# Flamingo block, one core: the second cross-attention's theta projection is moved to the input stage and kept in DRAM

## The chip, the cores and the metric

The kernel runs on one core of a Trainium2 chip. The metric is the device time of one execution in microseconds, the median of several runs. The profile is one execution recorded by the hardware. Its engines are TensorE (PE; its weight loads are PEld), VectorE (DVE), ScalarE (ACT), GpSimd (POOL) and SyncE (SP), which here only issues DMAs.

## What is computed

The block has four stages on `x` of 8 batches x 256 rows x 512 columns, with a context `ctx_2048` of the same shape. Each adds its gated result to x.

```python
x = x + tanh(g_xattn[0]) * L0_xattn(ctx, ctx, layernorm(x), ssm_kernel, D, 8)
x = x + tanh(g_ffn[0])   * L0_ffn(layernorm(x), w1, b1, w2, b2)          # int8-like, GELU
x = x + tanh(g_xattn[1]) * L1_xattn(layernorm(x), ctx, ...)
x = x + tanh(g_ffn[1])   * L1_ffn(x, w1, g1, w2, g2, w3, g3)             # ternary weights
```

The third line is the one that the change touches (input1 is the normalised x, input2 is the context, per batch 256 x 512):

```python
theta_x = einsum('ld,bdt->btl', theta_w, input2) + theta_b
phi_x   = einsum('ld,bdt->blt', phi_w, input1) + phi_b[:, None]
scores  = einsum('btl,bls->bts', theta_x, phi_x)
p       = softmax(scores, axis=-1)
g_x     = einsum('ld,bdt->btl', g_w, input1) + g_b
t_x     = einsum('bts,bsl->blt', p, g_x)
h       = relu((t_x - mean) * rsqrt(var + eps) * ln_gamma + ln_beta)     # mean, var over t and l
return einsum('ol,blt->bot', out_w, h) + out_b[None, :, None] + input2
```

`theta_x` depends on the context and two weights alone, not on x.

## The kernel before

The program is written out by hand for each engine, with semaphores between them. Each engine runs its own list of instructions in order, and a wait holds up all that stands behind it on that engine. There are 16 tiles of 128 rows (two to a batch), each 128 x 512 in float32, and 8 PSUM banks of 128 x 512.

**Input stage.** SyncE issues x and ctx in four groups of four tiles, 1 MB each (L306, L307), between them the small inputs (L309 to L312), then the convolution kernel's store to DRAM (`kpad_d`, L315), two bias loads (L316, L317) and the four 1 MB pieces of the first feed-forward's weights (L323). The third and fourth of these overwrite ctx in SBUF, so they wait until GpSimd has reversed its tiles (`c_rev`). For each tile t GpSimd reverses a piece of ctx (L456), ScalarE normalises x (L607), TensorE transposes ctx (L972) and x (L978), ScalarE copies the first out of PSUM (L615) and VectorE the second (L1305). VectorE makes the statistics of a group (L1295) between its copies. Then VectorE finds the largest magnitudes of the weights (L1323), ScalarE quantises them in four chunks of four instructions (L632), GpSimd or VectorE casts them (L481, L1342), TensorE transposes them (L963) and VectorE copies them out (L1332). ScalarE also issues the first loads of the convolution's matrices (L641).

**Convolution**, first feed-forward: L998 is the convolution's matmul, the first instruction of the next stage on TensorE. These stages are not touched.

**Second cross-attention.** Its eight batches are pipelined by one. TensorE's body for batch b is: `project(b + 1)` with theta (L1129, two float32 matmuls that the trace shows as four), phi (L1134) and g (L1142); `out_proj(b - 1)` (L1200); transposes of the probabilities (L1153); the product with g (L1182); `scores(b + 1)` (L1149); a small matmul for the mean (L1194). ScalarE copies theta (L851) and phi (L853) out with their bias, does the relu (L863), copies the transposed probabilities (L872) and takes the exponentials (L858). VectorE: statistics and normalisation of batch b + 2 (L1527, L1532, L1537), g out of PSUM (L1583), the residual (L1627, L1633), statistics of the product (L1601 to L1607), row maxima of the scores (L1589), the layer norm (L1612 to L1620), division of the exponentials (L1594, L1596). The weights of the four projections are loaded (L385, L386) and transposed (L1098) just before the stage, the context is loaded a second time (`ctx3`, L375), and the ternary weights are transposed between (L963, L1564 to L1569). `project(0)` stands among these.

**Names.** `arena` is one SBUF block out of which most tensors are cut, `turn`, `late` and `cols3` are further ones, `ps` is PSUM. `c_tr` and `q_tr` count transposed tiles of ctx and x, `c_out` and `q_out` copied ones, `pj_ready` finished projections, `th_out` copied projections, `sc_ready` finished score banks.

## Time and profile before

| | |
|---|---|
| median of 3 runs | 825.09 us (824.92 to 825.59) |
| span of the profiled execution | 821.3 us |
| TensorE busy | 680.4 us, 83% |
| VectorE busy | 707.5 us, 86% |
| ScalarE busy | 546.6 us, 67% |
| GpSimd busy | 359.2 us, 44% |
| input stage, up to the convolution's first matmul | 55.15 us |
| second cross-attention, theta(0) to the last scores | 465.5 to 590.3 us |

The span is from the first to the last instruction of one execution. The profiled execution's own time is not among the runs shown, and the distance from its span to the median of the runs is 3.8 us. Busy shares are averages over stages with different limits, so they are read by stretch. Where an instruction waited, its row in the timeline ends in brackets: the idle time before it, and who ended it. The start of DMA issues is also in the timeline, on SPq or ACTq. How long a transfer takes from its issue to its landing is in the DMA tables.

### The profile page before, as it was taken

Reading aid. Unit: us, or ns where it says so; the run is one execution under the profiler, and the core shown is the slowest. Engines: PE = TensorE matmul, PEld = TensorE weight load, DVE = VectorE, ACT = ScalarE, POOL = GpSimd, SP = SyncE. Lnnn points to the kernel's source line nnn. Section 1 sums busy time; section 2 is a strip of 40 time slices with the busy share of each in tenths; the row PEclk is TensorE's granted clock in tenths of the full one; section 3 lists DMA queues with packets and bytes.
Section 4 is the critical chain, followed back from the end, with each engine's and each line's share of the span. In section 5 each row is a group of like instructions: output and inputs, shape, how many; then the busy total and the mean of one; then the engine's idle time right before and its main releaser. Section 6 shows DMA issues by size and latency. Waiting matters only on the chain.

```text
span 821.3 us, 11803 instructions
## 1 busy us (share of the span) xinstructions
PE 680.4 (83%) x3440; PEld 405.8 (49%) x3476; DVE 707.5 (86%) x1044; ACT 546.6 (67%) x880; POOL 359.2 (44%) x436
## 2 busy tenths in 40 slices
PE   3669777597778738998969789999888999999996
PEld 3457555475555534443424655555534444444442
DVE  3867999999999974897789668888999999999993
ACT  3757777357677466989663554444557888888884
POOL 4649666387672240011753301010145556555552
PEclk9969999899999887998989999999999999999999
DMA  8925656077776220212865200000000000000000
GB/s 310 324 104 179 202 179 206 26 215 219 228 220 217 103 102 1 91 64 83 328 204 158 78 1 2 0 0 0 0 1 14 23 15 26 13 26 13 26 26 27
DMA packets 50048, 83.18 MB, mean 101 GB/s; under 512 B 6433, under 2 KB 19489, under 8 KB 48865
## 3 DMA queue, kind: packets, MB, share of 16 engines
q1 hardware_dynamic: 45664, 74.43, 27.1%
q10 hardware_dynamic: 4352, 8.39, 3.5%
q8 instruction: 14, 0.23, 0.1%
q14 instruction: 18, 0.14, 0.1%
HBM read 68.04 MB, written 14.76 MB: 101 GB/s over the span
## 4 chain that ended last, share of the span: by engine, by line
DVE 39%; PE 31%; ACT 12%; issue 12%; POOL 2%; DMA 2%; DVEq 1%; SPq 0%; ACTq 0%; POOLq 0%
DVE arena L1367 14%; PE ps L1075 5%; DVE turn L1360 5%; PE ps L1040 4%; ACT arena L922 3%; PE ps L1182 3%; PE ps L1149 3%; DVE arena L1646 3%; DVE q L1651 2%; PE ps L1129 2%; DVE arena L1734 2%; PE ps L1142 2%; PE ps L1134 2%; PE ps L1153 1%; DVE sw L1323 1%
## 5 line engine op out<-in xcount | busy, mean ns | idle before, releaser
L998 PE MATMUL ps<-arena 128*128 128x288 f32 x640 | 165.4, 417 | 44.8 <-ACT arena L670 33.5
L998 PEld LDWEIGHTS ps<-arena 128*128 128x128 f32 x640 | 122.3, 194 | 87.6 <-ACT arena L670 30.2
L1367 DVE TENSOR_REDUCE arena<-turn 128x2048 f32 (+1 forms) x32 | 123.8, 3872 | 0.0
L1220 PE MATMUL ps<-arena 128*128 128x512 bf16 x496 | 114.0, 380 | 10.7 <-ACT arena L898 7.6
L567 POOL TENSOR_TENSOR arena<-arena 128x512 f32<-128x512 f32 x64 | 87.8, 1374 | 68.9 <-DVE arena L1734 68.8
L473 POOL TENSOR_TENSOR arena<-arena 128x1024 f32<-128x1024 f32 x32 | 63.2, 1976 | 52.3 <-PE ps L998 51.7
L1220 PEld LDWEIGHTS ps<-arena 128*128 128x128 bf16 x512 | 47.5, 98 | 71.4 <-issue 14.2
L1075 PE MATMUL ps<-arena 128*128 128x512 bf16 x251 | 60.0, 402 | 10.8 <-DVE arena L1523 7.9
L1357 DVE TENSOR_TENSOR turn<-arena 128x1280 f32<-128x1280 f32 x32 | 53.5, 1671 | 14.7 <-ACT arena L670 12.6
L1238 PE MATMUL ps<-arena 128*128 128x512 bf16 x248 | 61.1, 386 | 0.8 <-ACT arena L914 0.5
L658 ACT ACTIVATE arena<-arena 128x512 f32<-128x512 f32 (+1 forms) x32 | 20.0, 629 | 60.0 <-DVE turn L1360 59.9
L1040 PE MATMUL ps<-arena 128*128 128x512 bf16 (+1 forms) x249 | 57.0, 385 | 2.3 <-ACT arena L769 1.7
L902 ACT ACTIVATE arena<-ps,q 128x512 f32<-128x512 f32 x64 | 41.7, 674 | 14.8 <-PE ps L1220 14.8
L1734 DVE SCALAR_TENSOR_TENSOR arena<-ps,q,arena 128x512 f32<-128x512 f32 x64 | 47.5, 744 | 0.7 <-ACT arena L902 0.5
L1075 PEld LDWEIGHTS ps<-arena 128*128 128x128 bf16 x256 | 25.9, 102 | 44.5 <-issue 17.7
L769 ACT ACTIVATE arena<-ps,b,s 128x512 f32<-128x512 f32 x64 | 45.3, 794 | 3.8 <-PE ps L1040 2.7
L858 ACT ACTIVATE arena<-ps,nmx 128x512 f32<-128x512 f32 x32 | 21.8, 685 | 33.7 <-DVE nmx L1589 33.0
L1740 DVE TENSOR_REDUCE q<-arena 128x1 f32<-128x512 f32 x64 | 42.1, 676 | 1.7 <-POOL arena L567 1.6
L908 ACT ACTIVATE arena<-arena,q 128x1024 int16<-128x1024 f32 x32 | 35.0, 1141 | 12.3 <-DVE q L1753 12.3
L1443 DVE TENSOR_REDUCE hmax<-arena 128x1 f32<-128x2048 f32 x15 | 34.0, 2277 | 9.9 <-ACT arena L769 9.9
L1040 PEld LDWEIGHTS ps<-arena 128*128 128x128 bf16 x256 | 24.9, 99 | 32.5 <-ACT arena L769 3.1
L667 ACT ACTIVATE arena<-ps 128x1024 f32<-128x1024 f32 x32 | 32.2, 1008 | 11.1 <-PE ps L998 11.1
(206 smaller groups left out, 1499.4 us busy)
## 6 DMA issues: line engine op xcount, KB each, us to landing
arena<-in_L_ffn_w SPq DMA_DIRECT2D x72, 256.0 KB, 4.2
arena<-kpad_d ACTq DMA_DIRECT2D x16, 512.0 KB, 4.5
late<-in_L_ffn_w SPq DMA_DIRECT2D x24, 256.0 KB, 4.3
tern_d<-late SPq DMA_DIRECT2D x48, 128.0 KB, 4.1
arena<-in_x SPq DMA_DIRECT2D x4, 1024.0 KB, 11.8
arena<-in_ctx SPq DMA_DIRECT2D x4, 1024.0 KB, 13.2
arena<-in_L_ffn_w SPq DMA_DIRECT2D x4, 1024.0 KB, 10.6
x_d<-arena SPq DMA_DIRECT2D x4, 1024.0 KB, 4.1
```

The costliest lines, as they stand in the source:

```text
L473: pool.tensor_tensor(dst[:, :, 0:32].rearrange("p r (d i) -> p r d i", d=4), a, shifted, ALU.mult)
L567: pool.tensor_tensor(hg[:, s, sl], hh[:, s, sl], g3[:, sl], ALU.mult).then_inc(S["hg_done"], 1)
L769: act.activation(hid[:, q, f, :], ps[:, f % 4, :], ACT.Gelu, bias=b1[:, f:f + 1], scale=s1[:, f:f + 1]).then_inc(S["gelu_done"], 1)
L998: last = pe.matmul(ps[:, 4 * s + lo, 0:NB * PAIRS], toep[:, u, (lo - li) * P:(lo - li) * P + P], kv[:, s, li, :], start=(li == 0), stop=(l ...
L1040: last = pe.matmul(ps[:, f % 4, :], fw1T[:, k, f * P:(f + 1) * P], xqT[:, k, ds(L * r, L)], start=(k == 0), stop=(k == LB - 1))
L1075: return pe.matmul(ps[:, 2 * j + f // 8, :], hq[:, r % 2, f, j * P:(j + 1) * P], fw2T[:, f, :], start=(f % 8 == 0), stop=(f % 8 == 7))
L1220: last = pe.matmul(ps[:, 3 + 2 * j + c % 2, :], xq4T[:, s, 4 * j + k, :], w[:, k, c * L:(c + 1) * L], start=(k == 0), stop=(k == LB - 1))
L1238: last = pe.matmul(ps[:, 7, :], hqT[:, f, :], bw3T[:, f, :], start=(f == 0), stop=(f == FT - 1))
L1357: v.tensor_tensor(prod[u][:, :, 0:5, :], bass.AP(yd.tensor, yd.offset, [yp, [YW, ROWS], [16, 5], [1, 8]]), bass.AP(qd.tensor, qd.offset, [ ...
L1367: v.tensor_reduce(qT[:, :, ds(HD * h, HD)], prod[u].rearrange("p r t i -> p r i t"), AX, ALU.add).then_inc(S["o_done"], 1)
L1734: v.scalar_tensor_tensor(out=hh[:, s, c * L:(c + 1) * L], in0=ps[:, 5 + c % 2, :], scalar=q4[:, 12 + 2 * s:13 + 2 * s], in1=sil[:, c, :], ...
L1740: dv.done(v.tensor_reduce(q4[:, 32 + c:33 + c], hg[:, s, c * L:(c + 1) * L], AX, ALU.max, apply_absolute_value=True))
```

## The change

- `theta_w` and `theta_b` are loaded behind the small inputs, ahead of the second group of x. TensorE transposes the two halves of theta_w after tile 1, and ScalarE copies them to `thw` after its copy of tile 2.
- `theta(b)` is computed on TensorE from the ctx that the input stage has in SBUF, after the transposes of tile 2b + 4, and for b = 6 and 7 at the end. It uses banks 1 to 3 in turn. ScalarE copies theta(b) with its bias to one of two buffers of `thT` (`th_copy`) after its copy of tile 2b + 5, and b = 6 and 7 at the end. From b = 2 on, this waits until the store of theta(b - 2) has landed (`th_moved`).
- SyncE stores the eight results to `th_d` in DRAM: 0 to 3 behind the second piece of the feed-forward weights, 4 and 5 behind the third, 6 and 7 behind the fourth. The third and fourth piece now also wait for the thetas that read the ctx tiles they overwrite.
- Before the second cross-attention theta(0) and theta(1) are loaded back; theta(b) for b of 2 and more is issued when the scores of b - 2 are done. `scores(b)` waits for the load. The projection and its copy are gone from there, and six weights are transposed there, not eight.
- GpSimd's first pairs of the convolution and the feed-forward's first weight transposes wait until theta is done with ctx and with the banks. Some semaphores are merged, to stay within their number, and `dynamic_dma_scratch_size` is set to 1024, which makes room in SBUF.

Cut to its core (numbers of semaphore counts that only shift are left out):

```diff
+        thT = sb("thT", [P, 2, L])
+        thw = sb("thw", [P, 4, P])
+        th_d = nc.dram_tensor("th_d", [NB, P, L], F32, kind="Internal").ap()
...
@@ SyncE, after the small inputs of group 0
+                    sp.dma_start(thw[:, 0:2, :], theta_w_d.rearrange("l (d k) -> l d k", d=2)).then_inc(S["w3_in"], 16)
+                    sp.dma_start(cols3[:, 0:1], theta_b_d.rearrange("(p o) -> p o", o=1)).then_inc(S["late_in"], 16)
...
+            def th_store(b):
+                sp.wait_ge(S["th_out"], b + 1)
+                sp.dma_start(th_d[b], thT[:, b % 2, :]).then_inc(th_moved[b % 2], 16)
+
             for c in range(4):
                 if c >= 2:
                     sp.wait_ge(S["c_rev"], G * (c + 1))
+                    sp.wait_ge(S["pj_ready"], 2 * c + 2)
                 sp.dma_start(raw[c].rearrange("p (j k) -> p j k", j=4), w1c[c]).then_inc(w_in[c], 16)
+                for b in ((), range(4), range(4, 6), range(6, 8))[c]:
+                    th_store(b)
...
+            def th_load(b):
+                sp.dma_start(thT[:, b % 2, :], th_d[b]).then_inc(th_moved[b % 2], 16)
+
+            for p in range(2):
+                sp.wait_ge(th_moved[p], 16 * NB // 2)
+            th_load(0)
+            th_load(1)
...
+            for b in range(2, NB):
+                sp.wait_ge(S["sc_ready"], 4 * (b - 1))
+                th_load(b)
...
@@ GpSimd
             pool.wait_ge(S["c_out"], NT)
+            pool.wait_ge(S["pj_ready"], NB)
...
@@ ScalarE
+            def th_copy(b):
+                act.wait_ge(S["pj_ready"], b + 1)
+                if b >= 2:
+                    act.wait_ge(th_moved[b % 2], 16 * (b // 2))
+                act.activation(thT[:, b % 2, :], ps[:, 1 + b % 3, :], ACT.Identity, bias=cols3[:, 0:1]).then_inc(S["th_out"], 1)
+
...
                 normalise_tile(x0[:, t % 4, :], t, t, S["xn0_ready"])
                 c_copy(t)
+                if t == 2:
+                    act.wait_ge(S["w3_tr"], 1)
+                    act.activation(thw[:, 2:4, :].rearrange("p a b -> p (a b)"), ps[:, 0, 0:2 * P], ACT.Copy).then_inc(S["w3_out"], 1)
+                    act.wait_ge(S["late_in"], 16)
+                if t >= 5 and t % 2 == 1:
+                    th_copy((t - 5) // 2)
+            for b in (NB - 2, NB - 1):
+                th_copy(b)
...
             def proj_out(b, p):
-                act.wait_ge(S["pj_ready"], 3 * b + 1)
-                act.activation(thT[:, p, :], ps[:, 0, :], ACT.Identity, bias=cols3[:, 0:1])
...
@@ TensorE
+            def theta(b):
+                pe.wait_ge(S["w3_out"], 1)
+                pe.wait_ge(c_in[b // 2], 16)
+                if b >= 3:
+                    pe.wait_ge(S["th_out"], b - 2)
+                for d in range(2):
+                    last = pe.matmul(ps[:, 1 + b % 3, :], thw[:, 2 + d, :], ctx_nat[:, 2 * b + d, :], start=(d == 0), stop=(d == 1))
+                last.then_inc(S["pj_ready"], 1)
...
                 last.then_inc(S["q_tr"], 1)
+                if t == 1:
+                    pe.wait_ge(S["w3_in"], 16)
+                    for d in range(2):
+                        last = pe.transpose(ps[:, 0, d * P:(d + 1) * P], thw[:, d, :], identf[:, :])
+                    last.then_inc(S["w3_tr"], 1)
+                if t >= 4 and t % 2 == 0:
+                    theta((t - 4) // 2)
+            for b in (NB - 2, NB - 1):
+                theta(b)
             for c in range(4):
                 pe.wait_ge(S["wqb_ready"], c + 1)
+                if c == 0:
+                    pe.wait_ge(S["th_out"], NB)
...
             def project(b, p):
                 pe.wait_ge(S["x3_done"], 2 * b + 2)
-                for d in range(2):
-                    last = pe.matmul(ps[:, 0, :], wT3[:, d, :], ctx3[:, ds(2 * b + d, 1), :].rearrange("p a t -> p (a t)"),
-                                     start=(d == 0), stop=(d == 1))
-                last.then_inc(S["pj_ready"], 1)
...
+            def scores(b, p, loaded):
+                pe.wait_ge(th_moved[p], 16 * (NB // 2 + loaded))
```

ScalarE in the input stage, tiles 7 to 9: before, a normalisation and a copy alternate.

```order
L615 ACTIVATE arena<-ps 128x4x128 [waits c_tr]
L607 ACTIVATE turn<-arena,shift2,rstd2 128x512 [waits q_tr,rs0]
L615 ACTIVATE arena<-ps 128x4x128 [waits c_tr]
L607 ACTIVATE turn<-arena,shift2,rstd2 128x512 [waits q_tr]
L615 ACTIVATE arena<-ps 128x4x128 [waits c_tr]
```

After, on the same engine for the same tiles (L628 is the normalisation, L636 the copy, L642 the copy of theta):

```order
L636 ACTIVATE arena<-ps 128x4x128 [waits c_tr]
L642 ACTIVATE thT<-ps,cols3 128x512 [waits pj_ready]
L628 ACTIVATE turn<-arena,shift2,rstd2 128x512 [waits q_tr,rs0]
L636 ACTIVATE arena<-ps 128x4x128 [waits c_tr]
L628 ACTIVATE turn<-arena,shift2,rstd2 128x512 [waits q_tr]
L636 ACTIVATE arena<-ps 128x4x128 [waits c_tr]
L642 ACTIVATE thT<-ps,cols3 128x512 [waits th_moved0,pj_ready]
```

A copy of theta now stands behind every odd tile, and the third one (the last row) also waits for a DMA, the first store.

SyncE's queue from the last group of ctx to the first ternary weights, before:

```order
L307 DMA arena<-in_ctx 128x4x512
L315 DMA kpad_d<-arena 32x640 [waits d_added]
L316 DMA b<-in_L_ffn_b 128x16x1
L317 DMA b2b<-in_L_ffn_b 128x512
L323 DMA arena<-in_L_ffn_w 128x4x512 x2
L323 DMA arena<-in_L_ffn_w 128x4x512 [waits c_rev] x2
L332 DMA arena<-in_L_ffn_w 128x512 [waits c_tr]
```

And after (L332 is now the feed-forward weights, L326 the store of theta):

```order
L309 DMA arena<-in_ctx 128x4x512
L319 DMA kpad_d<-arena 32x640 [waits d_added]
L320 DMA b<-in_L_ffn_b 128x16x1
L321 DMA b2b<-in_L_ffn_b 128x512
L332 DMA arena<-in_L_ffn_w 128x4x512 x2
L326 DMA th_d<-thT 128x512 [waits th_out] x4
L332 DMA arena<-in_L_ffn_w 128x4x512 [waits pj_ready,c_rev]
L326 DMA th_d<-thT 128x512 [waits th_out] x2
L332 DMA arena<-in_L_ffn_w 128x4x512 [waits pj_ready,c_rev]
L326 DMA th_d<-thT 128x512 [waits th_out] x2
L343 DMA arena<-in_L_ffn_w 128x512 [waits c_tr]
```

The stores stand between the weight loads, and the third and fourth load wait for finished thetas too.

## Rows read from the trace of the kernel before

**Rows 1.** Chain of waits, four stretches: start us, us, what it was spent on.

```profile
4.01 9.64 DMA arena<-in_x
...
465.67 1.77 PE ps L1129 x4
...
542.96 0.12 PE ps L1194 x2
543.08 1.82 PE ps L1129 x4
...
558.73 0.12 PE ps L1194 x2
```

**Rows 2.** Timeline, attention: start us, us, engine, line, operation, idle before.

```profile
543.00 0.69 DVE L1589 TENSOR_REDUCE nmx<-ps 128x1 f32<-128x512 f32 x1 [0.17 <-PE ps L1149]
...
547.66 0.48 DVE L1596 TENSOR_SCALAR arena<-arena,rrec 128x512 f32<-128x512 f32 x1
...
550.70 1.00 DVE L1537 TENSOR_SCALAR arena<-arena,mv,rstd 128x512 f32 x2 [0.50 <-POOL rstd L430]
...
553.16 1.41 DVE L1633 SCALAR_TENSOR_TENSOR arena<-turn,tg,arena 128x512 f32 x2
555.34 0.70 DVE L1601 BATCH_NORM_STATS2 bn<-ps 128x6 f32<-128x512 f32 x1 [0.77 <-PE ps L1182]
```

**Rows 3.** Busy time of a stretch: last three are clock, DMA share, GB/s.

```profile
32.50:35.00 2.50, 2.19 (x17) 1.72 (x17) 1.19 (x2) 2.50 (x5) 1.24 (x2) 1.00 1.05 404
```

**Rows 4.** Timeline, input stage: TensorE's and ScalarE's instructions for tiles.

```profile
20.72 0.60 PE L978 MATMUL ps<-identf,turn 128*128 128x128 f32 x4
...
27.91 0.58 ACT L615 ACTIVATE arena<-ps 128x512 f32<-128x512 f32 x1
...
28.39 0.81 ACT L607 ACTIVATE turn<-arena,shift,rstd 128x512 f32<-128x512 f32 x1
...
35.00 0.66 PE L978 MATMUL ps<-identf,turn 128*128 128x128 f32 x4
...
35.49 0.60 PE L972 MATMUL ps<-identf,arena 128*128 128x128 f32 x4
```

**Rows 5.** Timeline, from the last tile to the convolution's first matmuls.

```profile
36.14 0.59 ACT L615 ACTIVATE arena<-ps 128x512 f32<-128x512 f32 x1
...
36.64 0.48 ACTq L641 DMA_DIRECT2D arena<-kpad_d  x1
...
40.49 7.68 ACT L632 ACTIVATE turn<-arena,iw 128x512 int16<-128x512 f32 x12 [3.67 <-DVE iw L1327]
...
48.30 0.74 DVE L1342 CAST turn<-turn 128x2048 bf16<-128x2048 int16 x1
...
55.15 11.24 PE L998 MATMUL ps<-arena 128*128 128x288 f32 x39 [1.71 <-DVE arena L1332]
```

**Rows 6.** VectorE's waits from 495.7 to 590.3: us in total, times, longest.

```profile
DVE bn L1601 <- PE ps L1182: 3.6, 5, 0.9
...
DVE nmx L1589 <- PE ps L1149: 1.0, 6, 0.2
```

**Rows 7.** DMA issues by target: count, KB each, median us to landing.

```profile
out_x<-arena SPq DMA_DIRECT2D x16, 256.0 KB, 2.0
...
turn<-in_L_ffn_w SPq DMA_DIRECT2D x2, 1024.0 KB, 4.8
...
kpad_d<-arena SPq DMA_DIRECT2D x1, 80.0 KB, 12.2
...
gates<-in_g_xattn SPq DMA_DIRECT2D x1, 1.0 KB, 7.4
```

**Rows 8.** Timeline of SyncE's queue: the issue of b2b.

```profile
18.53 8.62 SPq L317 DMA_DIRECT2D b2b<-in_L_ffn_b  x1
```

**Rows 9.** L323's first two loads: issue ns, starts, then landing min/median/max.

```profile
L323 SPq DMA_DIRECT2D arena<-in_L_ffn_w x2: 435/704/972, 27.2 to 27.7; - x2
...
DMA to landing us min/median/max: 7.1/8.5/10.0
```

More of the change, by code:

```diff
@@ L127, in flamingo_gated_block @@
         xnb = cut(64, 2 * 2 * L).rearrange("p (s d l) -> p s d l", s=2, d=2)
-        thT = cut(72, 2 * L).rearrange("p (s t) -> p s t", s=2)
         phx = cut(76, 2 * L).rearrange("p (s t) -> p s t", s=2)
@@ L248, in flamingo_gated_block @@
         w_in = [sem(f"w_in{s}") for s in range(4)]
-        w2_in = [sem(f"w2_in{s}") for s in range(2)]
+        th_moved = [sem(f"th_moved{s}") for s in range(2)]
         traw_in = [sem(f"traw_in{s}") for s in range(4)]
@@ L353, in _ @@
                 sp.wait_ge(tint_out[c], 16 * 3 * FT // 4)
-            sp.dma_start(raw2[0], w2c[0]).then_inc(w2_in[0], 16)
+            sp.dma_start(raw2[0], w2c[0]).then_inc(w_in[0], 16)
             for g in range(NG):
@@ L367, in _ @@
                     sp.wait_ge(S["w2_used"], c - 1)
-                sp.dma_start(raw2[c % 2], w2c[c]).then_inc(w2_in[c % 2], 16)
+                sp.dma_start(raw2[c % 2], w2c[c]).then_inc(w_in[c % 2], 16)
             for g in range(NG):
@@ L382, in _ @@
                          tern_d[2].rearrange("r p n -> p r n")).then_inc(tern_in[1], 16)
-            for j, w in enumerate((theta_w_d, phi_w_d, g_w_d)):
+            def th_load(b):
[4 more added lines that the diff above has]
+            th_load(1)
+            for j, w in ((1, phi_w_d), (2, g_w_d)):
                 sp.dma_start(w3raw[:, 2 * j:2 * j + 2, :], w.rearrange("l (d k) -> l d k", d=2)).then_inc(S["w3_in"], 16)
             sp.dma_start(w3raw[:, 6:8, :], out_w_d.rearrange("(o p) l -> p o l", o=2)).then_inc(S["w3_in"], 16)
-            sp.dma_start(cols3[:, 0:1], theta_b_d.rearrange("(p o) -> p o", o=1)).then_inc(S["late_in"], 16)
             sp.dma_start(cols3[:, 1:2], phi_b_d.rearrange("(p o) -> p o", o=1)).then_inc(S["late_in"], 16)
@@ L409, in _ @@
             pool.nop().then_inc(S["kv_ready"], 2)
-            pool.memset(kpad[:, 0:NPAD], 0.0).then_inc(S["kz"], 1)
-            pool.memset(identf[:, :], 0.0).then_inc(S["ident_zeroed"], 1)
-            pool.memset(identb[:, :], 0.0).then_inc(S["ident_zeroed"], 1)
+            po.done(pool.memset(identf[:, :], 0.0))
+            po.done(pool.memset(identb[:, :], 0.0))
+            pool.memset(kpad[:, 0:NPAD], 0.0).then_inc(S["consts_set"], 1)
             pool.memset(mean_w[:, :], 1.0 / P).then_inc(S["consts_set"], 1)
@@ L418, in _ @@
                 pool.memset(rms_w[:, n:n + 1], value).then_inc(S["consts_set"], 1)
-            pool.wait_ge(S["ident_zeroed"], 2)
+            po.wait()
             for m in (identf, identb):
@@ L831, in _ @@
                     act.activation(ath[:, :], ath[:, :], ACT.Ln).then_inc(S["ath_ready"], 1)
-            act.wait_ge(S["w3_tr"], 1)
-            act.activation(wT3[:, :, :].rearrange("p a b -> p (a b)"), ps[:, 0:2, :].rearrange("p a b -> p (a b)"),
-                           ACT.Copy).then_inc(S["w3_out"], 1)
+            act.wait_ge(S["w3_tr"], 2)
+            act.activation(wT3[:, 2:8, :].rearrange("p a b -> p (a b)"),
+                           ps[:, 0:2, :].rearrange("p a b -> p (a b)")[:, 2 * P:8 * P], ACT.Copy).then_inc(S["w3_out"], 1)
             act.wait_ge(S["late_in"], 7 * 16)
@@ L955, in _ @@
             pe.nop().then_inc(S["y_ready"], 2)
-            pe.wait_ge(S["consts_set"], 8)
+            pe.wait_ge(S["consts_set"], 9)
             def weight_T(up, src, dst):
@@ L1096, in _ @@
             pe.wait_ge(S["w3_in"], 64)
-            for n in range(8):
+            for n in range(2, 8):
                 last = pe.transpose(ps[:, n // 4, (n % 4) * P:(n % 4 + 1) * P], w3raw[:, n, :], identf[:, :])
@@ L1106, in tern_T @@
                 if k == 3:
-                    pe.wait_ge(S["w3_out"], 1)
+                    pe.wait_ge(S["w3_out"], 2)
                 if k >= 4:
@@ L1144, in project @@
                 last.then_inc(S["pj_ready"], 1)
-            def scores(b, p):
-                pe.wait_ge(S["th_out"], b + 1)
+            def scores(b, p, loaded):
+                pe.wait_ge(th_moved[p], 16 * (NB // 2 + loaded))
+                pe.wait_ge(S["th_out"], NB + b + 1)
                 for k in range(4):
@@ L1186, in attn_body @@
                 if nxt:
-                    scores(b + 1, 1 - p)
+                    scores(b + 1, 1 - p, loaded)
                 if nxt:
@@ L1196, in out_proj @@
             def out_proj(b, copied):
-                pe.wait_ge(S["th_out"], copied)
+                pe.wait_ge(S["th_out"], NB + copied)
                 pe.wait_ge(S["relu_done"], b + 1)
@@ L1206, in _ @@
                 pe.wait_ge(*brought_out(k, S["bT_act"], S["bT_dve"], tern_on_dve))
-            scores(0, 0)
-            attn_body(0, 0, True, False)
+            scores(0, 0, 1)
+            attn_body(0, 0, True, False, 1)
             with pe.Fori(0, NB // 2 - 1) as i:
                 for u in range(2):
-                    attn_body(2 * i + 1 + u, (1 + u) % 2, True, True)
+                    attn_body(2 * i + 1 + u, (1 + u) % 2, True, True, i + 2)
             attn_body(NB - 1, 1, False, True)
@@ L1581, in gx_copy @@
             def gx_copy(b, p):
-                v.wait_ge(S["pj_ready"], 3 * b + 3)
+                v.wait_ge(S["pj_ready"], NB + 2 * b + 2)
                 v.tensor_tensor(gx[:, p, :, :], ps[:, 2, :].rearrange("p (b l) -> p b l", b=4),
```

14 lines of the change are left out of this document (7 added, 7 removed).

## The prediction

> **What bounds the kernel now.** I read the page's slices first, then the chain of waits, then two stretches instruction by instruction: the input stage (0 to 55 us), which the change loads, and the second cross-attention (465 to 590 us), which it relieves.
>
> In the attention stage the chain runs on TensorE alone: from one batch's last small matmul (L1194) to the next is 558.73 - 542.96 = 15.77 us, and inside it the theta projection (L1129) takes 1.82 us; the first projection, among the weight transposes, 1.77 us [rows 1]. So the first guess for what is taken off is 8 x 1.8 = 14 us. But VectorE is nearly as full: in the same period it waits 0.77 us at L1601 for TensorE's product and 0.17 us at the last row maximum (L1589); the 0.50 us at L1537 is a wait for GpSimd and stays [rows 2].
>
> The input stage is the other end. The DMA engines bring in 8 MB of x and ctx and 4 MB of weights, at full share and 404 GB/s where the queue is never empty [rows 3], and the normalise, transpose, copy-out loop over 16 tiles takes 35.00 - 20.72 = 14.28 us for ten tiles, 2.86 us for two [rows 4]. After it ScalarE quantises the first feed-forward's weights, and the long convolution starts at 55.15 us [rows 5]. From there on every stage waits for the one before, so each us that this start is late stays in the time.
>
> **The change, part by part.**
>
> *Taken out of the attention stage.* Projections 0 and 1: 1.77 + 1.7 us. Both are on TensorE's chain, and the engines behind it have room (VectorE's work of attention body 0 is light), so 3.5 us are gained before body 1. In bodies 1 to 6 TensorE alone could go from 15.77 to about 14.0 us. VectorE's chain decides instead. From the fourth row maximum (543.00) to the end of the residual update (553.16 + 1.41) are 11.57 us with its fixed wait in it; the next L1601 could start there, at 554.5, where it now starts at 555.34 [rows 2]. From L1601 on, the row maxima lose only their 0.17 us. So a period gives back its VectorE idle and no more: over 495.7 to 590.3 us that is 3.6 us at L1601 and 1.0 us at L1589 [rows 6], 4.6 us in six bodies, not 10.6. TensorE then waits for the normalised probabilities: they are ready 547.66 + 0.48 - 543.00 = 5.1 us after the fourth row maximum begins [rows 2], and it now waits for them where it waited for nothing. Sum: **-8.1 us**. ScalarE's eight theta copies there go too, but it waits anyway. The loads th_load(b) are issued two scores ahead, some 28 us, and 256 KB lands in a few us [rows 7]: nothing. Two transposes fewer of the attention weights lie beside the end of the second feed-forward matmul: nothing. The merged constant semaphores, and the smaller DMA scratch, which no DMA of this kernel uses: nothing.
>
> *Put into the input stage.* (a) Two more DMAs before the second x group. Its issue is now at 4.01 us behind six others, so one issue costs at most 0.67 us, and its landing (9.64 us later) starts the chain of the input stage [rows 1]. I take 1.0 us, between 0.3 and 1.5.
>
> (b) TensorE computes theta(b) after the transposes of tile 4, 6, ... 14, and ScalarE copies it out after each odd tile. This ties two tiles into one loop: transpose of the even tile (0.49 us to the next issue), theta 1.72, transposes of the odd tile of ctx 0.60, wake-up 0.05, the copy-out (27.91 to 28.39) 0.48, theta's copy-out of 128x512 with a bias, 0.6 from start to start by that same row, then the next even tile's normalisation 0.81 [rows 4], 0.05 again. Together 4.8 us for two tiles against 2.86. Transposes of tile 8 would then be at 20.72 + 1.0 + 2 x 4.8 = 31.3 us, and ScalarE ready for theta's third copy at 31.3 + 3.3 = 34.6.
>
> (c) That third copy needs the first store done (two thT buffers). SyncE issues the store behind b2b, which blocks the queue from 18.53 for 8.62 us [rows 8], and two 1 MB loads issued at 27.2 and 27.7 us, which landed 7.1 and 10.0 us later, the second at 37.7 [rows 9]. Is the store behind them in time as well as in order? Every small transfer in this queue was: 1 KB took 7.4 us, the 80 KB store kpad_d 12.2 us, behind megabytes [rows 7]. So the first store lands at 37.7 + 1.0 + 0.7 = 39.4 us and ScalarE stands 4.8 us, with the tiles behind it, and through them the transposes, VectorE's copies of q and GpSimd's reversals. The 0.7 us is 256 KB at the 404 GB/s of rows 3.
> The Trainium skill ("DMA: Bandwidth & Descriptors", Anatomy of one DMA) fits a transfer by itself as about 2.0 us plus its bytes at 436 GB/s, an estimate of 2.6 us for 256 KB; by that alone the store would be done at 32 us and step (c) would be nothing. The same page (Queues, rings and completion order) says that on each DMA engine descriptors are consumed in ring order, which is what the rows of small transfers show, so the sum goes by the rows.
>
> (d) From the stall: transposes of tile 10 at 39.4 + 0.6 + 0.8 + 0.05 = 40.9, tile 14 at 50.5 (now 35.00), theta(5) ends at 52.7. Only then may SyncE issue the third weight load, since it overwrites ctx, and the fifth store stands behind it: 52.7 + 4.8 (1 MB in an idle queue) + 0.7 = 58.2 us [rows 7]. Theta's last two copies wait for it and its neighbour: 59.4. Before, ScalarE's queue had issued its convolution loads (36.64 + 0.48) 0.4 us after the end of its last copy (36.14 + 0.59), so quantising starts at 59.8 to 59.9. Twelve pieces take 7.68 us: 67.6. VectorE's cast (48.30 before) follows, and the convolution starts 55.15 - 48.30 = 6.85 us after the cast: 74.4 us [rows 5]. Before, the quantising waited for VectorE's maxima; now those (10.6 us from 54.4) are done at 65. Sum: 74.4 - 55.15 = **+19.3 us**.
>
> *Total.* +19.3 - 8.1 = +11.2 us. The profiled execution spans 821.3 us, and the median of the runs is 825.09 us, 3.8 us round it that the change does not touch. Forecast: 821.3 + 11.2 + 3.8 = **836.3 us**.
>
> **The rivals.**
>
> 1. *The stores do not queue.* If a store issued at 28.5 us lands about 2.0 us later, as the output stores do in an idle queue [rows 7], (c) is zero. Tile 14 is then at 21.7 + 5 x 4.8 = 45.7, theta(5) ends at 47.9, the copies at 52.7 behind theta(7), the third quantised chunk at 60.8, the convolution starts at 67.7: +12.5, so 829.5 us. Against it stand the small transfers of 7 to 12 us. Chance 0.15.
>
> 2. *The attention stage gives all 14 us.* Then 836.3 - 6 = 830.3 us. It needs VectorE to lose what it does not lose in the diff; only its waits can go. Chance 0.06. Its opposite, in which TensorE's new wait for the probabilities and for the relu comes into VectorE's loop, gives 3.5 us only: 841 us. The relu is ready some 3.4 us after the fourth row maximum, TensorE wants it at 3.6, so this is near, but VectorE's path has over 1 us before it needs TensorE. Chance 0.07.
>
> 3. *Faster: theta disappears under the loads.* The input stage is fed by DMA, TensorE and ScalarE have gaps, and the convolution's start needs the weights more than the transposes. If the start is late only by (a), the time is 825.1 + 1.0 - 8.1 = 818 us. It turns faster if the input stage loses less than 8.1 us. For it: TensorE idles in that stage. Against it: the loop in (b) is fixed by the order on two in-order queues, and its sum without any stall, 5 x 1.94 = 9.7 us, is over 8.1. Chance 0.04.
>
> 4. *The change does less than it says*, losses and gains cancelling within 2 us: 0.02.
>
> **The numbers.** Forecast 0.66, rival 1 0.15, rival 2 0.06 and its opposite 0.07, rival 3 0.04, rival 4 0.02. The bounds of (a), of a wake-up more or less in (b) (5 x 0.2) and of the store's landing (1 us) give the forecast itself 833.5 to 839. The range reaches to rival 1 and to the opposite of rival 2: 829.5 to 841.5. Faster or slower counts from 0.2%, 1.7 us, about what a measurement of this kernel can tell from no change: faster 0.04, same 0.02, slower 0.94.
>
> **What would show it.** In the profile after: ScalarE idle about 5 us before theta's third copy, put down to a DMA; another wait before its seventh; two tiles every 4.8 us between; the convolution's first matmul near 74 us. In the attention stage: a period of 14.8 to 15.1 us, VectorE's wait at L1601's counterpart gone, and a TensorE wait of some 0.7 us before the transposes of the probabilities. It would be wrong if the first store lands long before 38 us, if the period stays above 15.3 or falls to 14.0, or if the later stages take up some of the late start.

## The result, and the profile after

The changed kernel takes 835.32 us (median of 4 runs, 834.12 to 836.22), the kernel before beside it 825.34 us (median of 4, 824.92 to 826.08): a ratio of 1.0112, 95% interval 1.0099 to 1.0126. It is slower by 10.0 us. The prediction was 836.3 us.

The profiled execution of after spans 834.4 us. The profiled runs here and below take 1.7 to 1.9 us more than their span (this one 836.22 us), so that of before, with 821.3 us, belongs to one of about 823.1 us, 2 us under its median. Where in a trace such differences come from is said in the last section.

The convolution's first matmul, of before (L998) and of after (L1051). After the colon stand min/median/max ns, then the first and the last start:

```profile
L998 PE MATMUL ps<-arena x640: 405/407/845, 55.2 to 263.2; 128*128 128x288 f32 x160
```

```profile
L1051 PE MATMUL ps<-arena x640: 406/406/844, 79.1 to 286.3; 128*128 128x288 f32 x160
```

The start moved from 55.2 to 79.1 us, +23.9. At the other end, the last matmul group of the attention gives way to the second feed-forward at 614.2 us, before at 601.3 us: of the lateness 12.9 us are left there. From the start of the first feed-forward's second matmul (384.2 us before, 407.9 after) to that point it is 217.1 us before and 206.3 after: the input stage lost 23.9 us, the attention won 10.8 back.

The chain of waits of after, input stage (start us, us, on what):

```profile
20.82 8.17 SPq L321
...
29.51 0.51 SPq L332
...
30.06 10.23 DMA th_d<-thT
...
40.37 0.69 ACT thT L642
41.06 0.71 ACT turn L628
...
41.81 1.11 PE ps L1020 x4
42.93 3.41 PE ps L1006 x4
...
56.40 0.40 SPq L332
...
56.84 6.43 DMA th_d<-thT
...
65.21 4.59 ACT turn L667 x8
```

L321 issues b2b, L332 the feed-forward weights, L326 the stores of theta, L642 is theta's copy, L628 a tile's normalisation, L1020 and L1014 are transposes of x and of ctx, L1006 is the theta product, L667 the quantising. As in [rows 8], b2b's issue blocks SyncE (8.17 us). The first store, behind it and two weight loads, lands 10.23 us after its issue, where the 256 KB output stores of [rows 7] take 2.0 us. ScalarE stands still for it, and TensorE behind ScalarE. TensorE's timeline and ScalarE's two waits:

```profile
27.41 0.66 PE L1020 MATMUL ps<-identf,turn 128*128 128x128 f32 x4 [1.09 <-ACT turn L628]
27.90 1.88 PE L1006 MATMUL ps<-arena,thw 128*128 128x512 f32 x4
...
32.18 0.66 PE L1020 MATMUL ps<-identf,turn 128*128 128x128 f32 x4 [1.09 <-ACT turn L628]
...
41.81 1.11 PE L1020 MATMUL ps<-identf,turn 128*128 128x128 f32 x4 [5.95 <-ACT turn L628]
42.72 3.62 PE L1006 MATMUL ps<-arena,thw 128*128 128x512 f32 x4
46.14 1.06 PE L1014 MATMUL ps<-identf,arena 128*128 128x128 f32 x4
...
49.16 0.66 PE L1020 MATMUL ps<-identf,turn 128*128 128x128 f32 x4 [0.94 <-ACT turn L628]
```

```profile
40.37 0.69 ACT L642 ACTIVATE thT<-ps,cols 128x512 f32<-128x512 f32 x1 [4.75 <-DMA th_d<-thT]
...
63.36 1.42 ACT L642 ACTIVATE thT<-ps,cols 128x512 f32<-128x512 f32 x2 [5.41 <-DMA th_d<-thT]
```

Two tiles take 32.18 - 27.41 = 4.77 us where nothing is stalled (2.86 before, [rows 4]). The pair behind the stall takes 49.16 - 41.81 = 7.35 us: after 5.95 us of idling, the granted clock is at the lower level, 1.2 GHz, and theta takes 3.62 us instead of 1.88. The row shows the busy time of each engine in that stretch; its last three numbers are the granted clock, the DMA share and GB/s:

```profile
41.80:47.00 5.20, 5.19 (x13) 3.00 (x14) 0.69 (x1) 1.15 (x2) 0.00 (x0) 0.50 0.13 50
```

In the attention, VectorE in one body of after, as [rows 2] of before (L1651 answers to L1601, L1639 to L1589):

```profile
556.24 0.69 DVE L1651 BATCH_NORM_STATS2 bn<-ps 128x6 f32<-128x512 f32 x1
...
557.38 2.48 DVE L1639 TENSOR_REDUCE nmx<-ps 128x1 f32<-128x512 f32 x4
...
562.05 0.49 DVE L1646 TENSOR_SCALAR arena<-arena,rrec 128x512 f32<-128x512 f32 x1
...
566.87 1.00 DVE L1587 TENSOR_SCALAR arena<-arena,mv,rstd 128x512 f32 x2 [0.50 <-POOL rstd L450]
...
569.33 1.41 DVE L1683 SCALAR_TENSOR_TENSOR arena<-turn,tg,arena 128x512 f32 x2
570.66 0.69 DVE L1651 BATCH_NORM_STATS2 bn<-ps 128x6 f32<-128x512 f32 x1
```

The period is 570.66 - 556.24 = 14.42 us, before 15.77. VectorE no longer waits for TensorE there, but for one wait of 0.2 us; its other waits from 516 to 602 us are for GpSimd, and TensorE's new one is for the normalised probabilities (in all, times, longest):

```profile
PEld ps L1203 <- DVE arena L1646: 3.0, 6, 0.5
...
DVE arena L1587 <- POOL rstd L450: 2.6, 5, 0.5
...
DVE arena L1670 <- POOL sm L552: 2.0, 6, 0.3
...
DVE nmx L1639 <- PE ps L1199: 0.2, 1, 0.2
```

The loads of theta take 2.7 us from issue to landing (median), issued two batches ahead; nobody waits for one.

### The profile page after: what moved, and what is told of

Its sections match the earlier page's. It is cut to its first block, busy times and chain, and to the rows that moved or that the text cites. A ratio compares the mean times of both kernels' runs of the same rounds, so it can differ in the third digit from the quotient of the medians.

```text
span 834.4 us, 11874 instructions
## 1 busy us (share of the span) xinstructions
PE 685.0 (82%) x3476; PEld 405.8 (49%) x3476; DVE 709.5 (85%) x1044; ACT 544.7 (65%) x881; POOL 358.3 (43%) x436
## 4 chain that ended last, share of the span: by engine, by line
DVE 36%; issue 24%; ACT 16%; PE 13%; SPq 3%; POOL 3%; DMA 2%; DVEq 1%; POOLq 0%; ACTq 0%
DVE arena L1417 13%; DVE turn L1410 4%; PE ps L1093 4%; ACT arena L955 3%; DVE arena L1696 3%; ACT turn L850 3%; PE ps L1051 2%; DVE q L1701 2%; DMA th_d<-thT 2%; ACT arena L804 2%; DVE arena L1784 2%; PE ps L1128 2%; ACT turn L914 1%; DVE turn L1602 1%; DVE arena L1809 1%
## 5 line engine op out<-in xcount | busy, mean ns | idle before, releaser
L1051 PE MATMUL ps<-arena 128*128 128x288 f32 x640 | 164.1, 414 | 45.2 <-ACT arena L705 33.5
L1051 PEld LDWEIGHTS ps<-arena 128*128 128x128 f32 x640 | 121.2, 192 | 87.8 <-issue 34.1
L1270 PE MATMUL ps<-arena 128*128 128x512 bf16 x512 | 116.2, 380 | 9.2 <-ACT arena L931 7.6
L1128 PE MATMUL ps<-arena 128*128 128x512 bf16 x256 | 61.0, 403 | 9.6 <-DVE arena L1573 6.9
L1288 PE MATMUL ps<-arena 128*128 128x512 bf16 x256 | 61.7, 386 | 0.1
L1093 PEld LDWEIGHTS ps<-arena 128*128 128x128 bf16 x256 | 24.8, 99 | 32.2 <-ACT arena L804 3.1
L1410 DVE TENSOR_TENSOR turn<-arena 128x768 f32<-128x768 f32 x32 | 39.6, 1237 | 0.0
```

What stands on the lines that cost most here:

```text
L1051: last = pe.matmul(ps[:, 4 * s + lo, 0:NB * PAIRS], toep[:, u, (lo - li) * P:(lo - li) * P + P], kv[:, s, li, :], start=(li == 0), stop=(l ...
L1093: last = pe.matmul(ps[:, f % 4, :], fw1T[:, k, f * P:(f + 1) * P], xqT[:, k, ds(L * r, L)], start=(k == 0), stop=(k == LB - 1))
L1128: return pe.matmul(ps[:, 2 * j + f // 8, :], hq[:, r % 2, f, j * P:(j + 1) * P], fw2T[:, f, :], start=(f % 8 == 0), stop=(f % 8 == 7))
L1270: last = pe.matmul(ps[:, 3 + 2 * j + c % 2, :], xq4T[:, s, 4 * j + k, :], w[:, k, c * L:(c + 1) * L], start=(k == 0), stop=(k == LB - 1))
L1288: last = pe.matmul(ps[:, 7, :], hqT[:, f, :], bw3T[:, f, :], start=(f == 0), stop=(f == FT - 1))
L1410: v.tensor_tensor(prod[u][:, :, 5:8, :], bass.AP(yd.tensor, yd.offset + 16 + 7, [yp, [YW, ROWS], [15, 3], [1, 8]]), bass.AP(qd.tensor, qd. ...
```

## The experiments

Every kernel is timed against before on the same chip. In the diffs, - is the changed kernel (in e1 and e8 the kernel before).

| kernel | us, median (runs) | before beside it | ratio, 95% | convolution from |
|---|---|---|---|---|
| after | 835.32 (4) | 825.34 | 1.0112 (1.0099 to 1.0126) | 79.1 |
| e1 before, small scratch | 826.26 (12) | 825.85 | 1.0001 (0.9990 to 1.0012) | 56.8 |
| e2 input half alone | 847.52 (4) | 825.85 | 1.0246 (1.0215 to 1.0278) | 78.8 |
| e3 attention half alone | 816.63 (4) | 825.85 | 0.9875 (0.9858 to 0.9893) | 57.8 |
| e4 eight buffers | 830.67 (6) | 825.85 | 1.0053 (1.0033 to 1.0074) | 71.3 |
| e5 stores on ScalarE's queue | 834.92 (5) | 826.76 | 1.0084 (1.0059 to 1.0109) | 78.0 |
| e6 a product more | 838.32 (4) | 826.76 | 1.0132 (1.0111 to 1.0153) | 78.1 |
| e7 eight buffers, weights later, normalise ahead | 823.08 (7) | 826.76 | 0.9960 (0.9946 to 0.9974) | 63.6 |
| e8 before, normalise ahead | 826.35 (10) | 826.20 | 1.0010 (0.9992 to 1.0027) | 56.3 |
| e9 eight buffers, weights later | 829.54 (8) | 826.20 | 1.0035 (1.0020 to 1.0051) | 70.5 |
| e10 two buffers, normalise ahead | 830.62 (6) | 826.20 | 1.0066 (1.0045 to 1.0087) | 71.2 |

### Does the smaller DMA scratch do anything?

The spans of before and after differ by 13.1 us, the medians by 10.0, so I first asked whether the smaller DMA scratch, a part of the change that I had set at nothing, plays a role.

```diff
-    nc = bacc.Bacc("TRN2", target_bir_lowering=False, num_devices=1)
+    nc = bacc.Bacc("TRN2", target_bir_lowering=False, num_devices=1, dynamic_dma_scratch_size=1024)
```

> The kernel before with the one setting dynamic_dma_scratch_size=1024 and nothing else. The span rose by 13.1 us (821.3 to 834.4) and the median of the runs by only 10.0, so some 2 to 3 us were saved outside the span. Theory: it is this setting; then this kernel is at 825.3 - 2 to 3 = 822.5 to 823.5 us with an unchanged span of 821.3. Rival: the profiled execution of before was a fast one, and the time outside the span is as before; then 825.3 us.

It measured no difference (1.0001, 0.9990 to 1.0012), so the theory fell. The setting is out, and the gap between spans and medians is execution to execution: this kernel's traced execution spans 826.0 us where that of before spans 821.3. Of these 4.7 us, 1.6 are a later start of the convolution (56.8 for 55.2 us) and 3.1 a longer convolution (211.1 for 208.0, last section). A stage start read off one trace is good to a microsecond or two.

### The two halves apart

e2 keeps the input half and projects in the attention as before:

```diff
-                pe.wait_ge(th_moved[p], 16 * (NB // 2 + loaded))
...
-                    pe.matmul(ps[:, 3 + k, :], thT[:, p, k * P:(k + 1) * P], phx[:, p, :],
+                    pe.matmul(ps[:, 3 + k, :], thA[:, p, k * P:(k + 1) * P], phx[:, p, :],
```

> The input half of the change alone: theta is computed, copied and stored while the inputs load, but never loaded back; the second cross-attention projects and copies it as before. Theory (the two halves add, the input stage costs 23.9 us and the attention stage gives 10.4): the time of the changed kernel plus 10.4, 845.7 us, with the convolution starting at 79 us. Rival (part of the late start is taken up by later stages, and the attention gives less than its traces seem to show): 843 us or less.

e3 takes every theta out of the input stage and fills its place in DRAM with other data, so its times are those of a kernel without this projection:

```diff
-                for b in ((), range(4), range(4, 6), range(6, 8))[c]:
-                    th_store(b)
...
-                if t >= 4 and t % 2 == 0:
-                    theta((t - 4) // 2)
```

> The attention half alone: no theta in the input stage. th_d is filled with 2 MB of x during the first feed-forward, so the attention works on wrong thetas (the theta projection is left out of the computation); loads, waits and instructions of the attention stage are those of the change. Theory: the convolution starts at 55.2 us and the time is 835.3 - 23.9 = 811.4 us, within 1 us. Rival (gain of 8.1 us as forecast, and a late start that costs less than it shows): 815 us.

By the ratios, 1.0246 and 0.9875, the halves are +20.3 and -10.3 us of 825.85; by the medians +21.7 and -9.2. Together that is +10.0 or +12.5, and the whole change has +10.0. With e2's interval, 2.6 us to either side, the halves add; a third effect of 2 us would not be seen. Both expectations missed in size. e2 was expected at 845.7 us and took 847.52, and e3 took 816.63 us, not 811.4, and more than the 815 us of its rival. So the 23.9 us between the two starts are too high a price for the input half: the changed kernel takes 18.7 us more than e3. In the traces its convolution starts 21.3 us later (79.1 for 57.8) and is 2.6 us shorter (207.2 for 209.8), which is the same 18.7.

e3's gain is still above the -8.1 us that I had for the attention; where the rest hides is in the traces: with theta back in the attention (e2) VectorE waits again as before, without it (e3) no more. VectorE's waits of e2 from 516 to 616 us, then of e3 from 497 to 583 us:

```profile
DVE bn L1652 <- PE ps L1233: 3.6, 5, 0.9
...
DVE nmx L1640 <- PE ps L1200: 1.2, 7, 0.2
```

```profile
DVE arena L1562 <- POOL rstd L445: 2.6, 5, 0.5
...
DVE nmx L1614 <- PE ps L1174: 0.2, 1, 0.2
```

### What bounds an attention body now?

e6 adds one matrix product, half of a theta projection, to each of the eight projections of the attention; its result isn't used.

```diff
+                pe.matmul(ps[:, 0, :], wT3[:, 2, :], ctx3[:, ds(2 * b, 1), :].rearrange("p a t -> p (a t)"), start=True, stop=True)
```

> The changed kernel with one more 128 x 128 x 512 float32 matrix product instruction on TensorE in each of the eight attention projections, 0.86 us each, half of a theta projection. Theory A (with theta away the scores came so early that VectorE is the bound of the first six attention bodies, the theta projection cost there only what stood behind VectorE): at most 0.4 us of each instruction is seen in a body, +1.5 to +3.5 us in all, two of the eight being the first two projections, which nothing hides: about 837 to 839 us. Rival B (TensorE's own row of instructions still sets the bodies): all of it is seen, 8 x 0.86 = +6.9 us, about 842 us.

The time is 838.32 us, 3.0 above the changed kernel's; against the kernel before beside each, it is 1.6 more (+11.6 for +10.0). In the traces, from the first scores to the second feed-forward, it is 617.0 - 499.3 = 117.7 us against 614.2 - 499.8 = 114.4: +3.3 us, of 6.0 us for the seven products that lie there. This is theory A and not B, which wanted all of it: nearly half of TensorE's extra work is hidden behind VectorE, the rest is not. The two engines are within half a microsecond of each other in a body.

### What do the stores cost, and why are they late?

e4 gives theta eight buffers, so that ScalarE waits for no store; the last three lie in late, which is free until the ternary weights.

```diff
-                if b >= 2:
-                    act.wait_ge(th_moved[b % 2], 16 * (b // 2))
-                act.activation(thT[:, b % 2, :], ps[:, 1 + b % 3, :], ACT.Identity, bias=cols3[:, 0:1]).then_inc(S["th_out"], 1)
+                act.activation(th_buf[b], ps[:, 1 + b % 3, :], ACT.Identity, bias=cols3[:, 0:1]).then_inc(S["th_out"], 1)
```

> The changed kernel with eight buffers for theta in SBUF, so that ScalarE's copy never waits for a store; the stores stay in SyncE's queue. Theory (the two waits for stores cost 4.75 and 5.4 us, and TensorE's half clock after the first some 2.5 us more): the convolution starts near 69 us and not at 79, so about 825.5 us. Rival (the waits hide behind VectorE's maxima and the late weight loads, which then end last): less than 5 us is gained, 831 us or more.

The convolution starts at 71.3 instead of 79.1 us and the kernel takes 830.67 us: 7.8 us of start, 4.7 us of time. Both expected numbers of the theory (69 and 825.5 us) were missed, and the rival's reason holds. The two waits are worth less than their 10.2 us. Without the second one ScalarE gets at the quantising early and then waits for VectorE's maxima of the last weights instead, whose load lands 8.76 us after its issue. About 1 us of the 7.8 may be the execution: e2 and e6 have the changed kernel's input stage and start at 78.8 and 78.1. ScalarE, e4:

```profile
53.32 7.45 ACT L667 ACTIVATE turn<-arena,iw 128x512 int16<-128x512 f32 x12 [0.38 <-issue]
...
63.90 2.56 ACT L667 ACTIVATE turn<-arena,iw 128x512 int16<-128x512 f32 x4 [3.12 <-DVE iw L1379]
```

The pairs keep their 4.8 us, as the step said: 4.77 us between TensorE's transposes of x, with a 1.09 us wait for ScalarE in each. TensorE, e4:

```profile
31.11 0.66 PE L1022 MATMUL ps<-identf,turn 128*128 128x128 f32 x4 [1.09 <-ACT turn L630]
...
35.89 0.66 PE L1022 MATMUL ps<-identf,turn 128*128 128x128 f32 x4 [1.09 <-ACT turn L630]
```

e5 keeps the two buffers and issues each store on ScalarE's queue, past SyncE's.

```diff
-                for b in ((), range(4), range(4, 6), range(6, 8))[c]:
-                    th_store(b)
...
+                act.wait_ge(S["th_out"], b + 1)
+                act.dma_start(th_d[b], thT[:, b % 2, :]).then_inc(th_moved[b % 2], 16)
```

> The changed kernel with its eight stores issued on ScalarE's own queue, right behind each copy, instead of SyncE's behind the weight loads. Theory (a store lands late because it stands in a ring behind weight loads that were issued before it): the first store lands 3 to 5 us after its issue instead of 10.2, ScalarE's waits for stores at the third and seventh copy fall from 4.8 and 5.4 us to under 1 us together, TensorE keeps its 2.4 GHz level there, the convolution starts near 71 us (with eight buffers and no wait it was 71.3, in the changed kernel 79.1), and the time is about 829 us. Rival (the DMA engines are full, and whatever queue it comes by, the store shares them): it lands 8 us or more after its issue, the waits stay above 3 us each, the convolution starts at 77 us or later, 834 us or more.

From issue to landing, e5's eight stores and, behind them, those of the changed kernel (L326):

```profile
L638 ACTq DMA_DIRECT2D th_d<-thT x8: 326/326/366, 26.5 to 58.9; - x8
...
DMA to landing us min/median/max: 2.0/3.8/7.4
```

```profile
L326 SPq DMA_DIRECT2D th_d<-thT x8: 320/320/516, 30.1 to 64.8; - x8
...
DMA to landing us min/median/max: 2.0/6.2/10.2
```

The stall at the third copy is gone and the median landing falls from 6.2 to 3.8 us. So the place in SyncE's order did make the first store late; that the DMA queue did is less clear. The first store of e5 is issued at 26.5 us, right behind its copy. In the changed kernel SyncE, busy with b2b and the two loads, issued it at 30.06. In e5 it is ahead of the weight loads (28.9 and 29.4 us) and lands after 3.9 us. The second is issued at 31.8 us beside these loads, which land at 36.1 and 40.1, and takes 7.4 us although it has a queue of its own. The Trainium skill ("DMA: Bandwidth & Descriptors", Queues, rings and completion order) has each DMA engine take turns between the queues that it has work for. The trace does not show that this frees a store from the loads of another queue: the one store that ran beside them took those 7.4 us. How the 10.23 us divide between the order in the queue and DMA engines shared with 2 MB of loads stays open. And the forecast of 829 us failed: 834.92 us, convolution at 78.0. The chain of e5 shows what took the place of the stalls:

```profile
52.39 0.69 ACT thT L636
53.10 4.68 DMA th_d<-thT
...
58.19 0.70 ACT thT L636
58.91 0.33 ACTq L638
59.49 3.98 ACTq L672
```

The last copy still waits 3.45 us for the sixth store. Each issue stands in ScalarE's own order, between theta's copy and the next normalisation, and makes a pair 33.11 - 27.75 = 5.36 us instead of 4.77. And the convolution's first load (L672), next in the same queue, blocks ScalarE for 3.98 us as it is issued; before, such an issue takes 0.48 us [rows 5]. The first store was freed, and its issuer paid.

### Can the pair be shorter?

A pair is long because ScalarE's theta copy and the even tile's normalisation stand between two of TensorE's pieces, while neither engine is full. e7 takes this apart: from the fifth tile on, ScalarE normalises one tile ahead. It also has e4's eight buffers, and the theta weights load behind the second pair of inputs.

```diff
+            def norm0(t):
...
             for t in range(NT):
-                normalise_tile(x0[:, t % 4, :], t, t, S["xn0_ready"])
+                if t <= 4:
+                    norm0(t)
+                if 4 <= t < NT - 1:
+                    norm0(t + 1)
                 c_copy(t)
```

> The changed kernel with eight buffers, the theta weights loaded behind the second pair of input loads instead of the first, and ScalarE normalising one tile ahead of the copy of a theta. Theory (the pair of tiles takes 4.8 us because ScalarE's theta copy and the next tile's normalisation stand in a row behind TensorE's theta and before its next transpose; neither engine is full): a pair falls to about 3.6 us, the first tile starts at 13.7 us again, the convolution starts at 61 to 64 us, and the time is 820 to 823 us, less than both kernels. Rival (TensorE's own work, or the order of VectorE's statistics, sets the pair): it stays at 4.5 us or more, the convolution starts at 70 us, 829 to 830 us as with eight buffers alone.

It takes 823.08 us, 0.9960 of before (0.9946 to 0.9974), less than both kernels. TensorE of e7 runs without a gap, 27.88 - 24.41 = 3.47 us for a pair (one of the pairs has a gap of 0.34 us and takes 3.99):

```profile
24.41 1.88 PE L1015 MATMUL ps<-arena,thw 128*128 128x512 f32 x4
...
27.88 1.88 PE L1015 MATMUL ps<-arena,thw 128*128 128x512 f32 x4
```

Is the order a gain by itself, and does it need the buffers? e8 has it on the kernel before (the same diff, on before's loop), e9 is e7 without it, e10 has it without the eight buffers.

> The kernel before, its theta projection left in the attention, with only the order of ScalarE changed: from the fifth tile it normalises one tile ahead of the copy of the context. It asks whether the order that helps the changed kernel is a gain by itself. Theory (before, a tile takes 2.86 us by several engines in turn and 1.7 us is ScalarE's work; no theta copy stands between a normalisation and the next transpose): within 1 us of before in the convolution's start (55.2 to 57.8 in the kernels that have no theta in the input stage) and in the time, 825 to 827 us. Rival (the order is a gain of its own, and the changed kernel with it owes its time to that, not to theta): the convolution starts at 53 us or earlier and the time is 823 us or less.

> The changed kernel with eight buffers and with the theta weights and bias loaded behind the second pair of input loads; ScalarE's order as in the changed kernel. Between the kernel with eight buffers alone (convolution from 71.3 us, 830.7 us) and the one that also normalises ahead (63.6 us, 823.1 us) it gives each its share. Theory: the first tile starts at 13.7 to 14.0 us instead of 15.6, the pairs still take 4.8 us, the convolution starts at 69 to 70 us, 828 to 829.5 us. Rival (the last tiles wait for the last input load anyway, which the two small loads delay wherever they stand): the first tile is earlier but the convolution still starts at 71 us or later, 830.5 us.

> The changed kernel with its two buffers and its early theta weights, and ScalarE normalising one tile ahead. Theory (the third copy is released by the first store, which lands at about 40.3 us because SyncE issues it at 30 us behind the weight loads, whatever the tiles do): the time won on the pairs before 40 us turns into a longer wait for that store, 6 to 8 us instead of 4.75, and only the pairs behind it are shorter; the convolution starts at 73 to 76 us, not the 66 us that the shorter pairs alone would give, and the time is 830 to 833 us. Rival (tiles and store shorten together): the third copy waits no longer than 5 us, the convolution starts at 71 us or earlier, 828 us or less.

e8 is the same as before (1.0010, 0.9992 to 1.0027; convolution from 56.3): the order pays only where theta's copy is in the row. e9 starts the first tile at 13.93 us (e4 at 14.57) and the convolution at 70.5, 0.8 us earlier than e4; in time 829.54 us. The expectation had a start of 69 to 70 and 828 to 829.5 us, the rival 71 or later and 830.5: the start lies between the two, the time at the theory's edge. So of e7's 7.7 us over e4 the order gives 6.9. In e10 the third copy waits 7.66 us, inside the 6 to 8 of the theory:

```profile
38.35 0.69 ACT L642 ACTIVATE thT<-ps,cols 128x512 f32<-128x512 f32 x1 [7.66 <-DMA th_d<-thT]
...
55.62 1.26 ACT L642 ACTIVATE thT<-ps,cols 128x512 f32<-128x512 f32 x2 [5.59 <-DMA th_d<-thT]
```

The time won on the tiles before the store turned into a longer wait for it. The time, 830.62 us, is in the theory's range. The convolution starts at 71.2 us, 2 us before its window: the store landed at 38.3 and not at 40.3 us, in an execution in which the first tile started 1.4 us earlier (14.24 us, after 15.63) and the two loads ahead of the store were issued 1.3 us earlier (27.70 and 28.18 us, after 29.03 and 29.51).

Together they divide the 23.9 us of the changed kernel's late start: buffers 7.8 (71.3 from 79.1), weights later 0.8 (70.5), ScalarE's order 6.9 (63.6); 8.4 us are left against before. Each is one trace against one trace, so the 0.8 is within what executions differ by (13.9 to 15.6 us for the first tile). What is left in e7 is on its chain: the fourth weight load may be issued only when the last theta has read the ctx that it overwrites.

```profile
41.56 3.45 PE ps L1015 x8
...
45.08 8.25 DMA arena<-in_L_ffn_w
...
53.34 2.30 DVE sw L1382
```

Whether another place for these weights gives more was not tried.

## Why the prediction was right

The time, 835.32 for 836.3 us, is nearer than the steps deserve, and part of that is luck. Both terms were too small, +19.3 for +23.9 and -8.1 for -10.8 us; in the spans this makes +13.1 where the sum said +11.2. The 1.9 us were taken back by another miss: I put 3.8 us round the span of before, as its distance from the median, where a run has 1.8, and the other 2.0 were that this one execution was fast.

- **Attention, -8.1 us.** The bound was named rightly: VectorE waits no more for TensorE, the period does not fall to 14.0 us, and TensorE waits for the probabilities (0.5 us each, 0.7 forecast). The first two projections gave 3.8 us (93.9 to 91.9 us from the second feed-forward matmul to the first scores, 10.5 to 8.7 from there to the first product) for 3.5. From there to the end it is 7.0 us instead of the 4.6 of six bodies. The term "a period gives back its VectorE idle and no more" was mis-sized: I read VectorE's idle off the waits that have a row. Four row maxima take 2.97 us before (a row of 2.12 for three, 0.17 idle, 0.69) and 2.48 after: the row of three had some 0.3 us of waits for the scores folded into it. The forecast of 14.8 to 15.1 us for the period was therefore too long; it is 14.42.
- **(a) The late x, +1.0.** Right on average (+1.1 us between the means of the two groups that follow), and uneven; in the traced execution of after it is +2.0, over the bound of 1.5: the first tile's statistics start at 13.67 to 14.06 us in six kernels that issue theta's weights later or not at all (before, e1, e3, e7, e8, e9), and at 14.24, 14.36, 14.57, 15.47, 15.47 and 15.63 in six that issue them first (e10, e6, e4, e2, e5, after).
- **(b) The pair, 4.8 us.** 4.77. And e7 confirms the reason: when the two copies leave TensorE's way, a pair is 3.47 us.
- **(c) The third copy waits for the store, ready at 34.6, landing 39.4, 4.8 us.** 4.75 us, ready at 35.6, released at 40.3. The wait and what it waits for are right; that it is 4.8 to a tenth is chance, since both ends came 1 us later (5.91 us in e6 and 4.52 in e2, with the same input stage). e5 and e4 show that the store is the cause, e5 only in part why it is late. Rival 1, in which the stores do not queue, fell. So did the 2.6 us of the estimate that stood beside the step; the fit that the Trainium skill gives there ("DMA: Bandwidth & Descriptors", Anatomy of one DMA) is for a transfer issued by GpSimd, and these are SyncE's.
- **(d) From there to the convolution, 74.4 us; it was 79.1.** Here 4.7 us are missing, and they are: 1.0 us from (a) and the later store; 2.6 us from the pair at the lower clock (7.35 for 4.77), which no step had; and 1.5 us at the second stall, where the third load and the fifth store took 63.3 - 56.4 = 6.9 us instead of 5.5. Against it, 0.4 us less from the cast to the convolution.
- **Rival 3,** that theta disappears under the loads, fell with the changed kernel; e7 shows what it takes to come nearer to it, and even then 8.4 us of the start stay.
- **"Each us that this start is late stays in the time."** Nearly so between the two traces: of the 23.9 us, 23.7 are there at the first feed-forward's second matmul. In general not: the kernels that reach the convolution at 78 us or later run it 0.6 to 4.2 us faster than the others (last section). The trace of before is the shortest of these others, so only 0.8 us of it lies between the two spans. One of the signs of being wrong, later stages that take up some of the late start, was therefore there in part, 18.7 us of time for 21.3 of start against e3.
- **The rest,** scratch and merged semaphores at nothing: e1 bears it out for the scratch.

## What to carry to other kernels

Work moved from a busy stage to one that looks idle can pay more for its place in the order of each in-order engine and queue it enters than for its size: here 8 x 1.7 us on a TensorE with gaps cost 23.9 us of start, of which the waits for stores and ScalarE's order, both removable, were 15.5 us (with the weights' place). Before such a move, write down the row of instructions on every engine around each insertion; where A waits for B's piece and B for A's, let one run a piece ahead, and give a store that stands behind megabytes of loads more buffers; another issuer won little here (e5 against e4). The gain at the other end is the idle of the next engine, and rows that merge several instructions (x3, x4) hide part of it: compare their length with the count times a single one.

## What the runs showed of the hardware

- A stall costs twice on TensorE. After 5.95 us of idling, a granted clock of 0.50 lasted for 5.2 us, and theta took 3.62 us for 1.88, +2.6 us on the pair. In e10 the lower level came after 5.74 us of idling; there it is the next three groups of transposes that took 1.06 to 1.11 us for 0.60 to 0.66, and theta 2.51 for 1.88. In e4 and e7, where tiles came without such a gap, theta kept its 1.88 us. A gap that long is not the only case: after's first theta took 2.24 us, in a stretch at 0.64 (20.2 to 24.8 us) behind 2.58 us of idling.
- The issue of a DMA can block its engine for long: b2b 8.17 us, and on ScalarE's queue 3.98 us for the convolution's first load behind e5's stores.
- The same instructions of the convolution stage take 206.9 to 207.4 us (first to last start) in the four traces that reach it at 78.0 us or later (after, e2, e5, e6), and 208.0 to 211.1 us in the other eight (before 208.0, e10 208.6, e7 209.0, e9 209.3, e8 209.6, e3 209.8, e4 210.4, e1 211.1). The granted clock goes with it: over the first 20 us of the stage, where TensorE is busy throughout, it is 1.00 in the four and 0.85 to 0.92 in the eight. In the two longest it is also below 1.00 over the next 40 us (e4 0.96, e1 0.91). The first 20 us of after, then of e4, columns as above:

```profile
79.10:99.10 20.00, 20.00 (x83) 15.70 (x84) 9.80 (x6) 13.35 (x35) 13.71 (x13) 1.00 0.42 131
```

```profile
71.30:91.30 20.00, 20.00 (x72) 15.37 (x73) 7.35 (x5) 10.96 (x28) 12.02 (x9) 0.87 0.27 87
```

These 20 us hold 83 matmuls in after and 72 in e4. The longer convolution is 3.1 of the 4.7 us between the spans of e1 and before. It is also why e4's 7.8 us of earlier start are 4.7 us in its time: its convolution is 3.2 us longer. In e4 the clock is still at the lower level when the stage begins; in after it has risen some 4 us before. Why it had risen in just the late ones no run shows.
